# Feed-forward of a one-core AdaLN + RWKV6 + FP4 kernel: silus placed ahead of ScalarE's other work, a third of h placed between two rounding steps, weight matrices transposed by DMA

## What is computed

```python
BLOCK = 16
_GRID = [0.0, 0.5, 1.0, 1.5, 2.0, 3.0, 4.0, 6.0]
_MID = [0.25, 0.75, 1.25, 1.75, 2.5, 3.5, 5.0]
def fp4_quant_dequant(x):               # along the last dim, in blocks of 16
    xb = x.reshape(shape[:-1] + (shape[-1] // BLOCK, BLOCK))
    scale = jnp.maximum(jnp.max(jnp.abs(xb), axis=-1, keepdims=True) / 6.0, 1e-12)
    idx = jnp.searchsorted(_MID, jnp.abs(xb / scale))
    q = _GRID[idx] * jnp.sign(xb / scale) * scale
    return q.reshape(shape)
def fp4_linear(x, w):                   # w_gate, w_up: 1408 x 512; w_down: 512 x 1408
    return jnp.einsum('bsk,nk->bsn', fp4_quant_dequant(x), fp4_quant_dequant(w))
...
h = _layernorm(x, axis=-1) * (1 + cb) + sb
gate, y = fp4_linear(h, w_gate), fp4_linear(h, w_up)
x = x + gb * fp4_linear(jax.nn.silu(gate) * y, w_down)
```

## Time and profile before

| | us |
|---|---|
| median of three runs | 4082.29 |
| the profiled execution, its own time | 4103.1 |
| span of the trace in it | 4100.9 |
| attention, to the barrier | 0 to 2480 |
| weights | 2480 to 2637 |
| loop of 64 tiles, with its start and end | 2637 to 4100.9 |

### The profile page before, as it was taken

The page is one execution under the profiler, slowest core; times in us unless marked ns, Lnnn a source line. Parts: engine busy times, 40 slices in busy tenths (PEclk is TensorE's granted clock), DMA queues, the critical chain, the costliest instruction groups (busy, mean ns, idle before and its releaser), DMA issues. The chain is left out here.

```text
span 4100.9 us, 151913 instructions
## 1 busy us (share of the span) xinstructions
PE 3687.1 (90%) x64072; PEld 2390.0 (58%) x64072; DVE 3323.2 (81%) x7542; ACT 1736.3 (42%) x3493; POOL 922.8 (23%) x737
## 2 busy tenths in 40 slices
PE   4999999999999998999999974299999999999998
PEld 3767767776676776767767752144444444444443
DVE  4778887887788887787878867788888888888887
ACT  2434434344353443443434413344444444444443
POOL 1122122221222212221222214422222222222221
PEclk7999999999999999999999986599999999999999
DMA  4000010000000000000000021023333333323323
GB/s 119 13 24 29 19 34 19 24 29 19 29 24 24 29 19 25 29 24 29 19 24 29 14 80 65 13 70 85 73 87 77 81 84 73 87 74 83 81 76 74
DMA packets 325484, 195.98 MB, mean 48 GB/s; under 512 B 265152, under 2 KB 265920, under 8 KB 324800
## 3 DMA queue, kind: packets, MB, share of 16 engines
q1 hardware_dynamic: 324800, 186.07, 16.8%
HBM read 89.56 MB, written 33.55 MB: 30 GB/s over the span
## 5 line engine op out<-in xcount | busy, mean ns | idle before, releaser
L782 POOL TENSOR_TENSOR raw_up<-raw_up,raw_gate 128x1024 f32<-128x1024 f32 x128 | 315.3, 2464 | 1180.4 <-DVE raw_up L832 1180.4
L950 DVE COPY_PREDICATED Am<-pick,banks 128x64 f32<-128x64 uint8 (+2 forms) x1792 | 461.2, 257 | 127.5 <-DVE Am L950 12.4
L1642 PE MATMUL fbank<-gT,xqT 128*128 128x464 f16 (+1 forms) x2304 | 490.1, 363 | 56.4 <-DVE h L1522 30.5
L1642 PE MATMUL fbank<-uT,xqT 128*128 128x464 f16 (+1 forms) x2304 | 487.6, 361 | 0.9 <-issue 0.8
L1651 PE MATMUL fbank<-dT,hqT 128*128 128x512 f16 x2112 | 468.9, 381 | 13.0 <-DMA hqT<-hq 12.9
L535 PE MATMUL banks<-raw_up,raw_gate 128*128 128x256 f32 x2048 | 456.8, 381 | 2.1 <-DVE xxx L845 2.1
L535 PEld LDWEIGHTS banks<-raw_up,raw_gate 128*128 128x128 f32 x2048 | 389.3, 191 | 67.6 <-issue 16.9
L1642 PEld LDWEIGHTS fbank<-gT,xqT 128*128 128x128 f16 x2304 | 216.9, 98 | 316.5 <-DVE h L1522 78.7
L436 PE MATMUL banks<-rcol,kvar 32*32 32x80 f32 x8192 | 337.8, 237 | 26.4 <-issue 25.9
L1642 PEld LDWEIGHTS fbank<-uT,xqT 128*128 128x128 f16 x2304 | 225.4, 98 | 232.6 <-issue 2.2
L1651 PEld LDWEIGHTS fbank<-dT,hqT 128*128 128x128 f16 x2112 | 206.5, 98 | 264.0 <-DMA hqT<-hq 16.6
(11 more groups left out here) (234 smaller groups left out, 7221.4 us busy)
## 6 DMA issues: line engine op xcount, KB each, us to landing
raw_scale<-in_L_attn_x SPq DMA_DIRECT2D x32, 512.0 KB, 3.8
xres<-in_L_attn_x SPq DMA_DIRECT2D x32, 512.0 KB, 3.7
x_after_attention<-xres SPq DMA_DIRECT2D x32, 512.0 KB, 2.9
xl<-x_after_attention SPq DMA_DIRECT2D x64, 256.0 KB, 2.7
xr<-x_after_attention SPq DMA_DIRECT2D x64, 256.0 KB, 2.6
out<-xr SPq DMA_DIRECT2D x64, 256.0 KB, 2.3
raw_gate<-in_L_ffn_w_gate SPq DMA_DIRECT2D x1, 2816.0 KB, 11.4
raw_up<-in_L_ffn_w_up SPq DMA_DIRECT2D x1, 2816.0 KB, 18.5
```

Source lines behind the costliest of these rows:

```text
L782: nc.gpsimd.tensor_tensor(xf[:, j % NXF].rearrange("p g b t -> p (g b) t"), xf[:, j % NXF].rearrange("p g b t -> p (g b) t"), hT[:, :, :, ...
L950: nc.vector.copy_predicated(dst, mask, src).then_inc((done or A_step).sem, 1)
L1642: last = nc.tensor.matmul(GU[2 * pair + t][:, 0:w], xqT[:, u, a, g, :], W[:, b_, g, lo_:hi_], start=(k == 0), stop=(k == 3 * G - 1))
```

## The change

Three edits, all in `feed_forward`:

1. `act_body` has another order: silu 1, grid x of n+1, silu 2, full x of n+1, statistics and ln of n+2, grid h of n, silu 0 of tile n+1, full h of n. A call ahead of the loop takes silu 0 of tile 0.
2. In `quantise`, `meanwhile()` (the first third of the next tile's h) stands between the two rounding steps instead of behind them.
3. Weights: ScalarE spreads both scale parts to full width (`full_scales`, two copies per item), VectorE multiplies q by them (`part_of`, two fp16 multiplications per item, one item later than q), and SP transposes the item's two parts with one DMA straight into gT, uT or dT. GpSimd's multiplications, TensorE's transposes, ScalarE's copies out of PSUM and the identity matrix are gone; GpSimd keeps its three reductions. The scale parts are split with 2^14+1 instead of 2^15+1, and two of the three wmod loads go to dT's memory at the start of the stage.

The diff, cut to its core:

```diff
-                    for m in range(1, 3):
-                        sp.wait_ge(a_done.sem, m * G)
-                        load_mod(m)
+                    for n, (t, r) in enumerate(items):
+                        if t == 2 and r == 0:
+                            sp.wait_ge(modf_done.sem, 6)
+                        sp.wait_ge(parts_done.sem, 2 * (n + 1))
+                        dst = (gT, uT, dT)[t][:, :, :, r * P:(r + 1) * P].rearrange("p a k n -> p (a k) n")
+                        sp.dma_start_transpose(dst, parts[:, n % 2, 0:2 * width(n)]).then_inc(wT_landed[n % 2].sem, 16)
+                        if n == G - 2:
+                            sp.wait_ge(a_done.sem, G)
+                            load_mod(2)
+                    for p in range(2):
+                        sp.wait_ge(wT_landed[p].sem, 8 * len(items))
...
+                    def full_scales(n):
+                        t, r = items[n]
+                        w, (view, spread) = width(n), blocks_of(n)
+                        act.wait_ge(scale_step.sem, scale_step.at(t))
+                        if n >= 2:
+                            act.wait_ge(parts_done.sem, 2 * (n - 1))
+                        for part, scale in enumerate((s_high, s_low)):
+                            nc.scalar.activation(view(full[:, n % 2, part, 0:w]), spread(scale, t % 2), ACT.Copy).then_inc(full_done.sem, 1)
...
+                    for t in range(3):
+                        pool.wait_ge(wmax_done.sem, t + 1)
+                        nc.gpsimd.partition_all_reduce(wall[:, t:t + 1], wmax[:, t:t + 1], P, bass.bass_isa.ReduceOp.max).then_inc(all_max.sem, 1)
...
+                    def part_of(n, part):
+                        w, p = width(n), n % 2
+                        dve.wait_ge(q_done.sem, n + 1)
+                        dve.wait_ge(full_done.sem, 2 * n + part + 1)
+                        if n >= 2:
+                            dve.wait_ge(wT_landed[p].sem, 16 * (n // 2))
+                        V.tensor_tensor(parts[:, p, part * w:(part + 1) * w], q16[:, p, 0:w], full[:, p, part, 0:w], ALU.mult).then_inc(parts_done.sem, 1)
...
                         V.scalar_tensor_tensor(a, m, GRID, a, ALU.max, ALU.add).then_inc(s_done.sem, 1)
+                        if n > 0:
+                            part_of(n - 1, 0)
                         dve.wait_ge(s_done.sem, n + 1)
-                        if n >= 2:
-                            dve.wait_ge(lo_done.sem, n - 1)
                         V.scalar_tensor_tensor(q16[:, p, 0:w], m, GRID, a, ALU.max, ALU.subtract).then_inc(q_done.sem, 1)
+                        if n > 0:
+                            part_of(n - 1, 1)
...
-            link(V.scalar_tensor_tensor(src, m, GRID, src, ALU.max, ALU.add))
-            link(V.scalar_tensor_tensor(q[:], m, GRID, src, ALU.max, ALU.subtract))
+            V.scalar_tensor_tensor(src, m, GRID, src, ALU.max, ALU.add).then_inc(step.sem, 1)
+            k[0] += 1
             if meanwhile:
                 meanwhile()
+            after(dve, step, n, k[0])
+            link(V.scalar_tensor_tensor(q[:], m, GRID, src, ALU.max, ALU.subtract))
...
         def act_body(act, j, u, n, do_m, do_out, more):
             if do_m:
+                act_silu(act, u, n, 1)
+            if more:
+                act_grid(act, n + 1, xstep, hx[:], mx[:], xgrid_done)
+            if do_m:
+                act_silu(act, u, n, 2)
+            if more:
+                act_full(act, n + 1, C, s16x, xs_done, full_x, xfull_done, xlow_done)
             if two_more(n):
+                act_stats(act, j + 1, u, n + 2)
                 act_ln(act, u, n + 2)
             if do_m:
                 act_grid(act, n, hstep, h[:, u], mh[:], hgrid_done)
+            if more:
+                act_silu(act, 1 - u, n + 1, 0)
+            if do_m:
                 act_full(act, n, I_FF, s16h, hs_done, full_h, hfull_done, hlow_done)
```

131 lines of the change are left out of this document (34 added, 97 removed).

## The result

The changed kernel takes 4012.95 us (median of four runs, 4011.56 to 4016.38); the kernel before, on the same chip, 4081.7 us (four runs, 4072.35 to 4091.49). The ratio is 0.9835, with a 95% interval of 0.9819 to 0.985: 69 us less, where 84 were predicted. In a later group of runs the changed kernel was measured again, with a ratio of 0.9849 (0.983 to 0.9868).

The account below looks back on a forecast made before the run. VectorE was taken as the loop's real limit, TensorE close behind; in the weights stage VectorE and GpSimd held each other up. Savings of 51 (loop) and 33 (weights) from 4082.3 us gave 3998, range 3978 to 4040.

Parts of the forecast that it names:

- Rival A: Loop: VectorE meets most of one GpSimd operation, 25 us more: 4023, chance 0.12; sign: turns 21.8, h divide above 2.5.
- D: Loop: silu 2 ahead of full x delays xq, kernel 4107 us, chance 0.04; sign: TensorE idle before each first slice.
- The 20.8 us between profiled execution and median: Whole kernel: profiled 4103.1 us against median 4082.29; the difference of 20.8 was said to lie outside the edits.
- Walk of the turn, silu part: Loop turn: silu 0 0.64 us, first third of h done at T + 6.6, needed at T + 9.6; slice 2's wait goes.
- Walk of the turn, VectorE's part: Loop turn: VectorE arrives 1.4 us earlier, xq done T + 17.0, DMA issued T + 17.1, landed 1.5 us before needed.
- one tail: Loop: VectorE meets only one tail of GpSimd's operations, about 0.4 us more, needing 21.1 per turn, under 21.4; in the forecast.
- First turn: Loop start: xq of tile 1 is late, second tile at 21.2 us instead of 16.5, a loss of 4.7.
- Weights, items: w_gate and w_up: 2.5 us per item, stretches 25.1 and 25.8 us instead of 35.95 and 34.53, 19.6 saved.
- Rival B: Weights stage: DMA landings of 5.0 instead of 2.8 us, items 3.3 apart, 17 us more: 4015; chance 0.08.
- Second reduction: Weights stage: VectorE's 5.60 us wait for GpSimd's second reduction goes, 5.6 us saved.
- w_down: Weights stage, w_down: four items 24.9 us, last DMA landing 4.8, total 31.1 against 42.07 us, 10.9 saved.
- Changeover: Behind the barrier: GpSimd changes from reductions to loop arithmetic, 6.00 us, partly hidden; cost between 0 and 6, taken as 2.

Follow-up runs that it names:

- the silus alone: Kernel before with only ScalarE's new order of silus, the third of h staying behind both rounding steps: 4035.9 us, ratio 0.991, 63 turns in 1366.8 us.
- the repeats: Kernel before and changed kernel, each unchanged and profiled again: 63 turns in 1402.9 and 1367.9 us; the changed kernel's ratio to before 0.9849.
- the small modulation: Changed kernel with GpSimd's layer norm multiplication and addition cut to 32 of 512 columns, the rest left out: ratio 0.9813 to before, 63 turns 1353.7 us.
- the quarters: Changed kernel with GpSimd's three 512-wide operations per turn each cut into four of 128 columns: ratio 0.9814 to before, 63 turns 1354.6 us.

## Why the prediction was right, and where it was off

The forecast was 3998 us, in a range of 3978 to 4040; the kernel took 4012.95, in the range and faster, as forecast. The direction and the stages were right, the size was too large. By stage 62 us came of 83.6, and that the medians came closer, 69 of 84, lies within the intervals of the ratios and is luck as far as the runs tell. Rival A, the lock with VectorE meeting most of one GpSimd operation (4023), is what happened in the loop, in a smaller form. Its sign was only half right: the turns came to 21.7, but the divide of h to 1.97 us and not above 2.5; most of the loss was in the scale of h. The sign of D, TensorE waiting for xqT ahead of the first slice, showed as well, but not D's cause: the landings kept their 2.8 us, and VectorE did not wait for full x.

**The 20.8 us between profiled execution and median** were put outside my edits. That was right: before's second profile was 29.8 us shorter than the first, and attention alone 29.8 shorter.

**Walk of the turn, silu part.** Right. The waits for silu 2 and at slice 2 are gone, and the silus alone bring 1366.8 us. What I gave to the third's new place was hardly needed: with silu 0 ahead of full h the third is nearly early enough even behind step two (the weight loads wait for it 10.9 us in 1250, before 69.4).

**Walk of the turn, VectorE's part.** This is the step that failed: "VectorE now arrives 1.4 earlier, no longer idle for silu 2". I let it keep all of the 1.4 us. But the new order brings VectorE's scale and divide of h onto the layer norm's two GpSimd operations. The instructions of the loop take VectorE 41.7 us longer than before, 0.66 a turn. So step one ended 7.2 us into the turn and not 5.8, xq 18.6 and not 17.0, its DMA was issued at 18.8 and not 17.1, and what should have had 1.5 us to spare came about when TensorE wanted it. Turns of 21.71 us instead of 21.4: 62 x 0.31 = 19, of which the 3 us that I had allowed for disturbances cover some. The loop gave 34.3 (35 from the repeats) instead of 51.

The sum of what VectorE needs shows what was mis-sized. I had 20.7 for before and 21.1 with one tail. Of the 20.7, 0.2 had been taken off as "a wait for full x", which misread: that row names VectorE's own q16x as the releaser, and the wait stayed (15.5 us in 58 turns). So before needed 22.3 - 1.4 = 20.9. To this come 0.66 for the longer instructions instead of my 0.4, and 0.14 of a new wait for VectorE's own q16h (8.3 us in 58 turns), since the third no longer stands behind the second step. That is 21.7, what was measured, and above TensorE's 21.38; in the changed loop VectorE waits for no other engine but once. By the same sum the small modulation (1.03 less) and the quarters (0.58 less) put it under 21.38, where the turns then were. I had named the mechanism; the mistake was to believe that VectorE would meet only "one tail". I had GpSimd's times and VectorE's shift in hand and did not lay them over each other for the new turn. On this point the Trainium skill (SBUF — State Buffer, "SBUF: two separate sides") says that the engine which starts first holds the shared port pair for its whole instruction, against a VectorE operation with two SBUF inputs or in a two-port mode. The 88-column operation that ended with GpSimd's multiplication agrees (1.21 us for 0.226 alone), and so do the quarters. The 9.70 us of one GpSimd multiplication beside 17 VectorE instructions are more than this rule for one instruction gives.

**First turn.** Predicted 21.2 us, measured 21.22. But one term was left out. TensorE stood idle for 5.07 us ahead of tile 1, and behind that its granted clock was lower: 0.78 from 2620.93 to 2627.15 us, and 0.52 over 6.2 us in the repeat, so that it stood at the lower of its two levels (1.2 of 2.4 GHz) for part or nearly all of these stretches, where before it was 1.00 behind an idle time of 0.67. The first 12 matmuls of tile 1 took 3.95 and 4.98 us instead of 2.60:

```profile
2620.93 3.95 PE L1618 MATMUL fbank<-gT,xqT 128*128 128x480 f16 x12 [5.07 <-DMA xqT<-xq]
```

That is what makes the second turn 22.75 us, and 24.29 in the repeat, instead of 21.4. With the first turn's old order the first two turns take 41.5 us together, where the changed kernel has 44.0 and 45.2 and before had 40.3; there tile 1 is held up at its slice 2 again (0.89 us, before 2.25).

**Weights, items.** The item of 2.5 us was right (GpSimd gone, durations of 0.68 and 0.42). 27.7 and 26.7 us instead of 25.1 and 25.8, of which my allowance of 1.5 covers a part; VectorE waited for landings 3.9 us in all:

```profile
DVE parts L1290 <- DMA gT<-parts: 2.4, 2, 1.9
...
```

The longest is the item behind the third load of wmod. Rival B, slow landings at every item, did not come; the landings of these DMAs have a median of 3.0 us, close to the 2.8 of the earlier trace rows. So the destination that is not contiguous costs little here. By an estimate from the figures of the Trainium skill (DMA: Bandwidth & Descriptors, "Latency and other measured facts") an item would take 0.3 us longer to transfer; the medians differ by 0.2.

**Second reduction.** Predicted 5.6, measured: the gap between the two stretches of items fell from 14.10 to 7.69 us, by 6.4.

**w_down.** 33.16 us instead of the 31.1 of my walk, so 8.9 saved and not 10.9. VectorE is not to blame: its last product ends at 2570.16 + 1.69 = 2571.85, 26.4 us into the stretch, where I had 26.1. The rest is the last DMA. VectorE's last products, and the four DMAs (duration ns min/median/max, first and last start):

```profile
2570.16 1.69 DVE L1290 TENSOR_TENSOR parts<-q,full 128x1408 f16<-128x1408 f16 x2 [0.63 <-DMA dT<-parts]
```

```profile
L1193 SPq DMA_TRANSPOSE dT<-parts x4: 3301/3320/3482, 2558.7 to 2572.9; - x4
...
DMA to landing us min/median/max: 5.2/5.2/5.4
```

SP takes 3.3 us for the issue, which I had not priced, and is still in the third when the last product is done, so that the fourth starts 1.0 us late, at 2572.9. Then come 5.2 to 5.4 us instead of my extrapolated 4.8, and some 0.4 to the barrier at 2578.60.

**Changeover.** 3.1 us instead of 2; the loop's first GpSimd operation came 8.0 us behind the barrier, where I had 6 to 7.

In sum 62 us (by stage) instead of 83.6: the loop 16 short, the weights and the start 4.6, the tail 0.4.

## What to carry to other kernels

Moving work to an earlier place in one engine's queue also moves every operation behind it, and so changes whom it meets. Where VectorE and GpSimd work side by side, lay the new times of both over each other before believing a gain. When GpSimd has time to spare and VectorE has not, cut GpSimd's long operations into short ones; it then waits instead of VectorE (13 us here). An operation that is put into an in-order queue "while we wait" must have its own input ready: the third of h was worth 4 us at most with its silu moved, and cost 103 without. And a short idle time of TensorE can cost more than its length, if its clock is lower behind it: 5.1 us idle cost 1.4 and 2.9 us more here.

## What was unexpected in the hardware

- Where GpSimd arithmetic (128x512 fp32, one behind the other) and VectorE's alternated, every VectorE operation was 1.07 us longer, fp32 and fp16 alike (0.68 to 1.75 us, 0.41 to 1.48): the price was the same for the longer and the shorter instruction.
- The other way round, VectorE instructions without a gap between them held up one GpSimd multiplication, 1.26 us by itself, so that it took 9.70 us and ended only when VectorE stood idle.
- How long a transposing DMA occupies the issuing engine grows with its blocks: 1.25 us for the 8 blocks of xqT, 1.4 for the 11 of hqT, 3.3 us for the 22 of w_down, where a plain load of x takes 0.3 to 0.6.
- GpSimd took 7.2 us to change from a reduction over all partitions to ordinary arithmetic, and 6.0 the other way. One unused operation on one column, put where GpSimd was idle, took 3 us off the start.
- The same loop code is 12 to 15 us (1%) slower behind another weights stage (1402, 1403 against 1414, 1417 us), and each of the two repeats its time. A part measured alone can hide a gain: the new weights stage saves 28 us by stage and 11 by ratio.
